# A two-layer MLP with per-row experts: the first chunks of the first layer by rows of x, with the weight loads spread over both queues

## The chip, the cores and the metric

The kernel runs on one NeuronCore of a Trainium2 chip. The metric is device time in microseconds (us), median over runs; an execution recorded by the hardware profiler gives the rows quoted here. Engines are named as in the profile: PE is the matrix engine (TensorE), PEld its weight loads, ACT ScalarE, DVE VectorE, POOL GpSimd, SP the sync engine, which here only issues transfers. SPq and ACTq are the transfers that SP and ACT issue.

## The reference

For 32 rows of x, each 256 tokens by 256 features, in fp32:

```python
h = gelu(einsum('bnd,hd->bnh', x, fc1_w) + fc1_b)         # HID = 1024, exact gelu
shared = einsum('bnh,sh->bns', h, fc2_w) + fc2_b          # 192 columns
We, be = experts_w[indices], experts_b[indices]           # one of 16 experts per row, 64 columns
expert_x = einsum('bnh,bph->bnp', h, We) + be[:, None, :]
return x + concatenate([shared, expert_x], axis=-1)
```

## The kernel before

Sixteen blocks of two rows of x (512 tokens) are worked on in turn. Hidden features lie in 8 chunks of 128. Every fp32 operand is split into two parts in a rounded fp32 format: a high part (HI), which ACT writes with a copy that rounds, and the rest (LO), which DVE or POOL writes as source minus HI. A product of two operands is three matmuls: HI HI, HI LO, LO HI. So each operand goes through a fixed relay: PE (or DVE, by 32x32 squares) transposes it into PSUM, ACT makes HI, DVE makes LO, and only then is it complete for PE.

Blocks 0 and 1 compute fc1 plainly, as 8 chunks each: a chunk is 2 halves of the features times 3 terms, 6 matmuls of 512 columns into one PSUM bank (`conv_chunk(c)`; `first_chunk()` for chunk 0 of block 0). Four banks are in turn, so chunk c waits for the gelu of chunk c-4. From block 2 on, fc1 runs in a Strassen-like scheme whose weight sums are made on POOL and DVE meanwhile. fc2 follows one pair of chunks behind: `fc2_first` for block 0, `fc2` later.

The order of work is written out by hand, one list for each engine, and each engine takes its list strictly in that order; semaphores join them. What counts for the change is the start:

- Loads. SP issues x of block 0 as two transfers (row 0, row 1; 256 KB each), waits for row 0, then issues the second half of fc1's weights (chunks 4 to 7, four strips of 128 KB), fc2's weights (`w2_piece`), the experts' rows and more. ACT issues the index, the first half of fc1's weights (chunks 0 to 3, four strips) and the bias b1.
- PE. `warm(20)` runs 20 matmuls on a constant, then 8 transposes of x (`x0_banks`; the PSUM banks are split by feature half, so both rows must be there before either bank is complete), `warm(10)`, 8 transposes of the first half of fc1_w (`w1_bank(0, d)`), b1, chunk 0, 8 transposes of the second half (`w1_bank(1, d)`), chunks 1 to 7, then `fc2_first(0)` (24 matmuls of 256 columns), then chunk 0 of block 1 (`conv_chunk(K)`).
- `fc2_first(0)` waits for `h_lo` (first pair of h split), for `e_lo` (experts' weights split, first half) and `w2_lo` 4 (all of fc2's weights split). `conv_chunk(K)` waits for `x1_lo` 2 (x of block 1 split).
- ACT and DVE make these splits between the gelus: `w1_high`/`w1_low`, `w2_square`, `w2_high`/`w2_low`, `both_experts_square`/`_high`/`_low`, `x_square`, `x1_high`/`x1_low`; `conv_high(q)` is the HI copy of h, one copy of 1024 elements for each pair of chunks.

In the trace, L1036 is `warm`, L1030 a transpose, L1074 `first_chunk`, L1067 `conv_chunk`, L1117 `fc2_first`; on ACT L456 x0_high, L469 w1_high, L479 w2_high, L498 both_experts_high, L510 x1_high, L560 the HI copy of h, L572 the gelu of a chunk; on DVE L716 w1_low, L739 w2_square, L747 w2_low, L775 and L782 the experts, L791 x_square, L808 x1_low, L886 to L891 drain_first, which frees fc2's accumulators for block 1.

## Time and profile before

| | |
|---|---|
| median of 3 runs | 360.57 us (360.05 to 361.18) |
| profiled execution, device time | 360.29 us |
| its span in the trace | 358.1 us |
| share of PE in the chain that ended last | 98% |
| PE busy / DVE / ACT / POOL | 98% / 73% / 69% / 66% |

Device time is the span and 2.2 us around it. The span is what the rows below describe, counted in us from its start. The busy time of PE is that of matmuls whose ends are modelled, so how far apart matmuls start says more than their durations.

### The profile page before, as it was taken

The numbers are of one execution on the slowest core, as the hardware profiler recorded it, in microseconds if no ns is written. First come the engines' busy times: TensorE is split into PE (matmuls) and PEld (weight loads), VectorE is DVE, ScalarE is ACT, GpSimd is POOL, SyncE is SP. The second block draws the span as 40 slices with busy tenths as digits, with TensorE's granted clock in tenths as the row PEclk, the third lists the DMA queues.
The fourth block names the chain that finished last, engine by engine and source line by source line (L and its number), as shares of the span: only waits on it lengthen the run. The fifth ranks groups of instructions, "written<-read, shape, count | busy, mean of one in ns | idle before, by whom it ended". The sixth has DMA issues, their size and how long they took to land.

```text
span 358.1 us, 7085 instructions
## 1 busy us (share of the span) xinstructions
PE 352.4 (98%) x2383; PEld 324.2 (91%) x2383; DVE 260.3 (73%) x500; ACT 246.6 (69%) x410; POOL 235.0 (66%) x150
## 2 busy tenths in 40 slices
PE   8999999999999999999999999999999999999995
PEld 6899899999999999999999999999999999999984
DVE  1797976977859698686968869697786959844543
ACT  3794957777677686776777678677767768656640
POOL 0079977858756587765758866586865658774570
PEclk9999999999999999999999999999999999999999
DMA  8969654524324333332533324234331231312001
GB/s 197 189 148 206 144 144 131 150 78 108 112 59 136 94 90 126 89 120 66 147 97 88 113 78 128 82 94 149 90 102 57 88 98 32 117 37 90 29 31 59
DMA packets 70061, 37.53 MB, mean 105 GB/s; under 512 B 43530, under 2 KB 70026, under 8 KB 70026
## 3 DMA queue, kind: packets, MB, share of 16 engines
q1 hardware_dynamic: 69408, 36.55, 38.0%
q10 hardware_dynamic: 618, 0.53, 0.6%
q8 instruction: 19, 0.31, 0.4%
q14 instruction: 16, 0.13, 0.1%
HBM read 28.68 MB, written 8.39 MB: 104 GB/s over the span
## 4 chain that ended last, share of the span: by engine, by line
PE 98%; DVE 0%; ACT 0%; issue 0%; POOL 0%; POOLq 0%; DVEq 0%
PE fc_ps L1091 39%; PE acc_ps L1147 30%; PE acc_ps L1150 15%; PE fc_ps L1067 6%; PE acc_ps L1117 3%; PE fc_ps L1036 2%; PE fc_ps L1147 1%; PE tr_ps L1030 1%; PE fc_ps L1150 1%; PE fc_ps L1074 1%; DVE resid L914 0%; ACT w1t L469 0%; PE acc_ps L1030 0%; POOL ident L416 0%; POOL ident L414 0%
## 5 line engine op out<-in xcount | busy, mean ns | idle before, releaser
L390 POOL TENSOR_TENSOR ht<-gelu,ht 128x1024 fp32r<-128x1024 f32 x62 | 149.5, 2412 | 98.8 <-ACT ht L560 98.8
L1147 PE MATMUL acc_ps<-w2t,ht 128*128 128x512 f32 x464 | 168.0, 396 | 0.0
L1091 PE MATMUL fc_ps<-xt,w1t 128*128 128x256 f32 x1176 | 159.6, 283 | 0.0
L1091 PEld LDWEIGHTS fc_ps<-xt,w1t 128*128 128x128 f32 x1176 | 148.6, 189 | 5.3
L1150 PE MATMUL acc_ps<-w2t,ht 128*128 128x256 f32 x464 | 130.0, 280 | 0.0
L1147 PEld LDWEIGHTS acc_ps<-w2t,ht 128*128 128x128 f32 x464 | 87.4, 188 | 16.0 <-POOL ht L390 0.3
L1150 PEld LDWEIGHTS acc_ps<-w2t,ht 128*128 128x128 f32 x464 | 87.8, 189 | 0.0
L560 ACT ACTIVATE ht<-gelu 128x1024 fp32r<-128x1024 f32 x64 | 68.0, 1063 | 3.3
L586 ACT ACTIVATE gelu<-work,b 128x512 f32<-128x512 f32 x56 | 37.3, 715 | 26.4 <-DVE work L865 26.2
L398 POOL TENSOR_TENSOR xt<-work,xt 128x1024 fp32r<-128x1024 f32 x14 | 33.8, 2415 | 14.9 <-ACT xt L549 14.9
L865 DVE TENSOR_TENSOR work<-fc_ps,work 128x512 f32<-128x512 f32 x28 | 19.4, 691 | 22.6 <-PE fc_ps L1091 21.3
L858 DVE TENSOR_TENSOR work<-fc_ps,work 128x512 f32<-128x512 f32 x28 | 19.1, 681 | 20.6 <-PE fc_ps L1091 20.6
L378 POOL TENSOR_TENSOR resid<-resid,bias 128x384 f32<-128x384 f32 x32 | 33.9, 1058 | 0.0
L489 ACT ACTIVATE w2t<-tr_ps 128x512 fp32r<-128x512 f32 x28 | 16.8, 599 | 24.6 <-DVE tr_ps L758 24.6
L539 ACT ACTIVATE work<-fc_ps 128x512 f32<-128x512 f32 x28 | 16.9, 602 | 21.8 <-PE fc_ps L1091 21.7
L914 DVE TENSOR_TENSOR resid<-acc_ps,resid 128x256 f32<-128x256 f32 x60 | 24.1, 422 | 8.2 <-PE acc_ps L1150 7.2
L873 DVE TENSOR_TENSOR work<-fc_ps,work 128x512 f32<-128x512 f32 x28 | 19.4, 691 | 13.2 <-PE fc_ps L1091 13.2
L795 DVE TENSOR_TENSOR work<-b_rows 128x256 f32<-128x256 f32 x14 | 27.7, 1976 | 1.2 <-ACT b_rows L530 1.1
L598 ACT ACTIVATE gelu<-work,b 128x256 f32<-128x256 f32 x56 | 25.4, 508 | 0.0
L907 DVE TENSOR_TENSOR resid<-acc_ps,resid 128x192 f32<-128x192 f32 x56 | 19.9, 355 | 6.8 <-PE acc_ps L1150 5.9
L603 ACT ACTIVATE gelu<-fc_ps,b 128x256 f32<-128x256 f32 x56 | 23.4, 475 | 0.0
L1067 PE MATMUL fc_ps<-xt,w1t 128*128 128x512 f32 x90 | 22.0, 392 | 0.0
(70 smaller groups left out, 326.6 us busy)
## 6 DMA issues: line engine op xcount, KB each, us to landing
pieces<-in_L_cond_experts_w SPq DMA_DIRECT2D x128, 64.0 KB, 2.0
out<-resid SPq DMA_DIRECT2D x32, 256.0 KB, 3.1
pieces<-in_x SPq DMA_DIRECT2D x60, 128.0 KB, 2.9
resid<-in_x SPq DMA_DIRECT2D x15, 512.0 KB, 3.5
e_bias<-in_L_cond_experts_b SPq DMA_DIRECT2D x32, 32.0 KB, 2.8
work<-in_L_cond_fc_w SPq DMA_DIRECT2D x4, 256.0 KB, 4.4
w_piece<-in_L_cond_fc_w SPq DMA_DIRECT2D x4, 192.0 KB, 5.2
resid<-in_x SPq DMA_DIRECT2D x2, 256.0 KB, 3.5
```

What stands on the lines that cost most here:

```text
L378: nc.gpsimd.tensor_tensor(rows[:, :, 0:SHARED], rows[:, :, 0:SHARED], bias[:, :].unsqueeze(1).to_broadcast([P, T, SHARED]), ALU.add).then_ ...
L390: nc.gpsimd.tensor_tensor(ht[:, slot, LO, :, :].rearrange("p k t -> p (k t)"), gelu[:, q % GELUS, :, :].rearrange("p k t -> p (k t)"), ht[ ...
L398: nc.gpsimd.tensor_tensor(xt[:, n % 2, X_T1:X_T4 + 1, LO, :], t_sum, xt[:, n % 2, X_T1:X_T4 + 1, HI, :].bitcast(FP32), ALU.subtract).then_ ...
L560: nc.scalar.activation(ht[:, q % SLOTS, HI, :, :].rearrange("p k t -> p (k t)"), gelu[:, q % GELUS, :, :].rearrange("p k t -> p (k t)"), A ...
L586: nc.scalar.activation(gelu[:, q % GELUS, j, :], upper[:, j, :], ACT.Gelu, bias=b1[:, k:k + 1]).then_inc(up_gelu, 1)
L598: nc.scalar.activation(gelu[:, q % GELUS, j, SEQ:2 * SEQ], c22[:, j, :], ACT.Gelu, bias=b1[:, k:k + 1]).then_inc(c22_gelu, 1)
L795: nc.vector.tensor_tensor(t_sum[:, o, :], in0, in1, ALU.subtract)\
L914: nc.vector.tensor_tensor(dst, src, dst, ALU.add).then_inc(drained, 1)
L1067: last = nc.tensor.matmul(fc1_ps[:, c % 4, :], conv_operand(k, d, w), xt_plain[c // K][:, d, v, :], start=(at == 0), stop=(at == len(terms ...
L1091: last = nc.tensor.matmul(fc1_ps[:, dst, j * SEQ:(j + 1) * SEQ], w1t[:, w, wv, ms], xt[:, n % 2, o, xv, :], start=(fresh and j == 0 and at ...
L1147: nc.tensor.matmul(acc.rearrange("p (v o) -> p v o", v=2), ht[:, q % SLOTS, HI, j, ts], w2t[:, :, k, fc2_columns(b)], start=(k == 0), stop ...
L1150: last = nc.tensor.matmul(acc[:, OUT:2 * OUT], ht[:, q % SLOTS, LO, j, ts], w2t[:, HI, k, fc2_columns(b)], start=False, stop=True, skip_gr ...
```

## The change

Only the start of the program is written anew.

- Loads: SP issues row 0 of x, then strips 0 and 1 of fc1's weights for chunks 0 and 1 (64 KB each), then four strips for chunks 2 and 3; ACT issues strips 2 and 3 for chunks 0 and 1 first, then row 1 of x, the index and b1. SP still waits for row 0 before the second half of the weights.
- PSUM banks are split by row of x and by chunk pair of the weights, not by feature half: `x0_banks(b)` fills one bank of row b with both feature halves, `w1_bank(half, l)` one bank with chunks 2l and 2l+1 of that half. The numbers of transposes (8 for x, 16 for fc1_w) and the sizes of the splits stay.
- PE: 12 warm matmuls instead of 20, and the 10 between x and the weights are gone. Chunks 0 and 1 are computed row by row (`first_chunk(c, b)`), 24 matmuls of 256 columns instead of 12 of 512. The transposes of the second half of the weights stand behind chunk 2.
- ACT: `conv_chunk(1)` stands between `w1_high(1, 0)` and `w1_high(1, 1)`; `conv_high(0)` stands ahead of `conv_chunk(2)`, where it stood behind `w2_high(3)`.
- DVE: the first two `w2_square` stand ahead of `w1_low(1, ...)`, where they stood behind.

```diff
-    WARM = 20
+    WARM = 12
...
-            for b in range(R):
-                ts = slice(b * T, (b + 1) * T)
-                sp.dma_start(resid[:, 0, ts, :], x_blocks[0][:, ts, :]).then_inc(x0_loaded[b], 16)
+            load_x0(sp, 0)
+            load_w1_pair(sp, 0, (0, 1))
+            load_w1_pair(sp, 1, range(Q))
...
+            load_w1_pair(act, 0, (2, 3))
+            load_x0(act, 1)
             act.dma_start(index_sb[:, :], index.rearrange("(o n) -> o n", o=1))\
                 .then_inc(index_loaded, 16)
-            load_w1(act, 0)
...
-            for d in range(D):
-                x0_high(d)
-            for d in range(D):
-                w1_high(0, d)
+            x0_high(0)
+            w1_high(0, 0)
+            x0_high(1)
+            w1_high(0, 1)
             act.wait_ge(b1_ready, 1)
             conv_chunk(0)
             w1_high(1, 0)
+            conv_chunk(1)
             w1_high(1, 1)
-            conv_chunk(1)
             w2_high(0)
             w2_high(1)
+            conv_high(0)
             conv_chunk(2)
             w2_high(2)
             conv_chunk(3)
             w2_high(3)
-            conv_high(0)
...
-            for d in range(D):
-                w1_low(1, d)
             w2_square(0)
             w2_square(1)
+            w1_low(1, 0)
+            w1_low(1, 1)
...
+            def first_chunk(c, b):
+                for at, (w, v, d) in enumerate([(w, v, d) for w, v in ((HI, HI), (HI, LO), (LO, HI))
+                                                for d in range(D)]):
+                    if c == 0 and at == 0:
+                        pe.wait_ge(w1_hi, 1)
+                        pe.wait_ge(x0_hi, b + 1)
+                    if c == 0 and (w, v, d) == (HI, LO, 0):
+                        pe.wait_ge(x0_lo, b + 1)
+                    if c == 0 and (w, v, d) == (LO, HI, 0):
+                        pe.wait_ge(w1_lo, 1)
...
             warm(WARM)
-            for b in range(R):
-                x0_banks(b)
-            warm(WARM // 2)
+            x0_banks(0)
             pe.wait_ge(w1_loaded[0], 16 * Q)
-            for d in range(D):
-                w1_bank(0, d)
+            w1_bank(0, 0)
+            x0_banks(1)
+            first_chunk(0, 0)
             pe.wait_ge(b1_loaded, 16)
             nc.tensor.transpose(fc1_ps[:, 3, 0:K], b1_in[:, :], ident[0:K, 0:K]).then_inc(b1_tr, 1)
-            first_chunk()
+            first_chunk(1, 0)
             pe.wait_ge(w1_loaded[1], 16 * Q)
-            for d in range(D):
-                pe.wait_ge(x0_lo, d + 1)
-                w1_bank(1, d)
-            conv_chunk(1)
+            w1_bank(0, 1)
+            first_chunk(0, 1)
+            first_chunk(1, 1)
+            pe.wait_ge(w1_lo, 2)
             conv_chunk(2)
+            pe.wait_ge(w1_loaded[2], 16 * Q)
+            pe.wait_ge(x0_lo, 2)
+            for l in range(2):
+                w1_bank(1, l)
             conv_chunk(3)
-            pe.wait_ge(w1_lo, 4)
+            pe.wait_ge(w1_lo, 3)
             conv_chunk(4)
             conv_chunk(5)
+            pe.wait_ge(w1_lo, 4)
```

PE's program from its first matmul to the end of fc2_first(0), before:

```order
L1036 MATMUL fc_ps<-ident 128x256 x20
L1030 MATMUL tr_ps<-ident,resid 128x128 x8
L1036 MATMUL fc_ps<-ident 128x256 x10
L1030 MATMUL acc_ps<-ident,w_in 128x128 x8
L1168 MATMUL fc_ps<-ident,b_in 128x8
L1074 MATMUL fc_ps<-xt,w1t 128x512 x6
L1030 MATMUL tr_ps<-ident,w_in 128x128 x8
L1067 MATMUL fc_ps<-xt,w1t 128x512 x42
L1117 MATMUL acc_ps<-w2t,ht 128x256 x24
```

and in the changed kernel, where L1046 is warm, L1040 a transpose, L1091 first_chunk, L1075 conv_chunk and L1130 fc2_first:

```order
L1046 MATMUL fc_ps<-ident 128x256 x12
L1040 MATMUL tr_ps<-ident,resid 128x128 x4
L1040 MATMUL acc_ps<-ident,w_in 128x128 x4
L1040 MATMUL tr_ps<-ident,resid 128x128 x4
L1091 MATMUL fc_ps<-xt,w1t 128x256 x6
L1180 MATMUL fc_ps<-ident,b_in 128x8
L1091 MATMUL fc_ps<-xt,w1t 128x256 x6
L1040 MATMUL acc_ps<-ident,w_in 128x128 x4
L1091 MATMUL fc_ps<-xt,w1t 128x256 x12
L1075 MATMUL fc_ps<-xt,w1t 128x512 x6
L1040 MATMUL tr_ps<-ident,w_in 128x128 x8
L1075 MATMUL fc_ps<-xt,w1t 128x512 x30
```

18 warm matmuls are gone (8 ahead of x, 10 ahead of the weights), and the last 8 transposes of weights have moved from behind chunk 0 to behind chunk 2.

ACT's program from the first split to the HI copies of the experts' weights, before:

```order
L456 ACTIVATE xt<-tr_ps 128x512 x2
L469 ACTIVATE w1t<-acc_ps 128x2x256 x2
L572 ACTIVATE gelu<-fc_ps,b 128x512
L469 ACTIVATE w1t<-tr_ps 128x2x256 x2
L572 ACTIVATE gelu<-fc_ps,b 128x512
L479 ACTIVATE w2t<-acc_ps 128x2x192 x2
L572 ACTIVATE gelu<-fc_ps,b 128x512
L479 ACTIVATE w2t<-acc_ps 128x2x192
L572 ACTIVATE gelu<-fc_ps,b 128x512
L479 ACTIVATE w2t<-acc_ps 128x2x192
L560 ACTIVATE ht<-gelu 128x1024
L572 ACTIVATE gelu<-fc_ps,b 128x512
L498 ACTIVATE w2t<-tr_ps 128x2x4x64 x2
```

and in the changed kernel (L481 x0_high, L485 w1_high, L496 w2_high, L577 the HI copy of h, L589 a gelu, L515 both_experts_high):

```order
L589 ACTIVATE gelu<-fc_ps,b 128x512
L485 ACTIVATE w1t<-tr_ps 128x2x256
L589 ACTIVATE gelu<-fc_ps,b 128x512
L485 ACTIVATE w1t<-tr_ps 128x2x256
L496 ACTIVATE w2t<-acc_ps 128x2x192 x2
L577 ACTIVATE ht<-gelu 128x1024
L589 ACTIVATE gelu<-fc_ps,b 128x512
L496 ACTIVATE w2t<-acc_ps 128x2x192
L589 ACTIVATE gelu<-fc_ps,b 128x512
L496 ACTIVATE w2t<-acc_ps 128x2x192
L589 ACTIVATE gelu<-fc_ps,b 128x512
L515 ACTIVATE w2t<-tr_ps 128x2x4x64 x2
```

The copy of 1024 elements stands two gelus and two w2_high earlier; the gelu of chunk 1 stands one w1_high earlier. Two x0_high and two w1_high stand in turn ahead of these rows.

DVE's program from the first split of weights to w2_low, before:

```order
L716 TENSOR_TENSOR w1t<-acc_ps,w1t 128x2x256 x2
L921 COPY b<-fc_ps 128x8
L716 TENSOR_TENSOR w1t<-tr_ps,w1t 128x2x256 x2
L739 STREAM_TRANSPOSE acc_ps<-w_piece 128x6x2x32 x2
L747 TENSOR_TENSOR w2t<-acc_ps,w2t 128x2x192
L739 STREAM_TRANSPOSE acc_ps<-w_piece 128x6x2x32
L747 TENSOR_TENSOR w2t<-acc_ps,w2t 128x2x192
L739 STREAM_TRANSPOSE acc_ps<-w_piece 128x6x2x32
L747 TENSOR_TENSOR w2t<-acc_ps,w2t 128x2x192 x2
```

and in the changed kernel (L726 w1_low, L749 w2_square, L757 w2_low):

```order
L726 TENSOR_TENSOR w1t<-acc_ps,w1t 128x2x256
L931 COPY b<-fc_ps 128x8
L749 STREAM_TRANSPOSE acc_ps<-w_piece 128x6x2x32 x2
L726 TENSOR_TENSOR w1t<-tr_ps,w1t 128x2x256 x2
L757 TENSOR_TENSOR w2t<-acc_ps,w2t 128x2x192
L749 STREAM_TRANSPOSE acc_ps<-w_piece 128x6x2x32
L757 TENSOR_TENSOR w2t<-acc_ps,w2t 128x2x192
L749 STREAM_TRANSPOSE acc_ps<-w_piece 128x6x2x32
L757 TENSOR_TENSOR w2t<-acc_ps,w2t 128x2x192 x2
```

The two w2_square that wait for the load of fc2's weights now stand ahead of the split of the second half of fc1's weights.

## Rows read from the trace of the kernel before

**Rows 1.** The page: span, and the chain that ended last by engine.

```profile
span 358.1 us, 7085 instructions
...
PE 98%; DVE 0%; ACT 0%; issue 0%; POOL 0%; POOLq 0%; DVEq 0%
```

**Rows 2.** Busy time by window: us, busy (count) of PE, PEld, DVE, ACT, POOL, granted clock, DMA, GB/s.

```profile
12.00:24.00 12.00, 12.00 (x65) 10.36 (x64) 10.72 (x19) 11.10 (x20) 4.83 (x2) 1.00 0.72 161
24.00:350.00 326.00, 326.00 (x2237) 302.27 (x2237) 243.48 (x465) 230.85 (x384) 229.43 (x142) 1.00 0.37 100
```

**Rows 3.** Timeline of PE, 0 to 24.9: start, us from first start to last end.

```profile
1.53 4.40 PE L1036 MATMUL fc_ps<-ident 128*128 128x256 bf16 x20 [1.53 <-POOL ident L416]
5.77 1.11 PE L1030 MATMUL tr_ps<-ident,resid 128*128 128x128 f32 x8
6.72 1.26 PE L1036 MATMUL fc_ps<-ident 128*128 128x256 bf16 x10
7.81 1.12 PE L1030 MATMUL acc_ps<-ident,w_in 128*128 128x128 f32 x8
...
9.14 1.83 PE L1074 MATMUL fc_ps<-xt,w1t 128*128 128x512 f32 x6
10.80 1.11 PE L1030 MATMUL tr_ps<-ident,w_in 128*128 128x128 f32 x8
11.66 9.81 PE L1067 MATMUL fc_ps<-xt,w1t 128*128 128x512 f32 x42
21.31 3.04 PE L1117 MATMUL acc_ps<-w2t,ht 128*128 128x256 f32 x24
24.18 1.09 PE L1067 MATMUL fc_ps<-xt,w1t 128*128 128x512 f32 x4
```

**Rows 4.** Timeline of ACT, 0 to 24.9.

```profile
6.74 1.09 ACT L456 ACTIVATE xt<-tr_ps 128x512 fp32r<-128x512 f32 x2 [1.72 <-PE tr_ps L1030]
...
16.91 0.49 ACT L479 ACTIVATE w2t<-acc_ps 128x384 fp32r<-128x384 f32 x1
17.30 1.05 ACT L560 ACTIVATE ht<-gelu 128x1024 fp32r<-128x1024 f32 x1
18.24 0.68 ACT L572 ACTIVATE gelu<-fc_ps,b 128x512 f32<-128x512 f32 x1
18.81 1.08 ACT L498 ACTIVATE w2t<-tr_ps 128x512 fp32r<-128x512 f32 x2
...
21.85 1.12 ACT L510 ACTIVATE xt<-tr_ps 128x512 fp32r<-128x512 f32 x2
```

**Rows 5.** Timeline of DVE, 0 to 24.9.

```profile
17.91 1.31 DVE L775 STREAM_TRANSPOSE tr_ps<-pieces 128x512 f32<-128x512 f32 x2
19.44 1.29 DVE L782 TENSOR_TENSOR w2t<-tr_ps,w2t 128x512 fp32r<-128x512 f32 x2 [0.22 <-ACT w2t L498]
20.77 1.32 DVE L791 STREAM_TRANSPOSE tr_ps<-pieces 128x512 f32<-128x512 f32 x2
22.52 1.29 DVE L808 TENSOR_TENSOR xt<-tr_ps,xt 128x512 fp32r<-128x512 f32 x2 [0.43 <-ACT xt L510]
```

**Rows 6.** Transfers of x, rows 0 and 1: duration of an issue, first and last start, landing.

```profile
L317 SPq DMA_DIRECT2D resid<-in_x x2: 443/450/458, 0.8 to 1.2; - x2
...
DMA to landing us min/median/max: 3.0/3.5/3.9
```

**Rows 7.** Transfers of fc1's weights; the landings are of all eight strips.

```profile
L267 ACTq DMA_DIRECT2D w_in<-in_L_cond_fc_w x4: 359/450/453, 1.3 to 2.7; - x4
...
DMA to landing us min/median/max: 3.2/4.1/4.3
```

**Rows 8.** Landing of fc2's weights (L322).

```profile
DMA to landing us min/median/max: 4.6/5.2/5.8
```

**Rows 9.** Timeline of all engines, 28 to 52: drain_first and block 1's fc2.

```profile
43.83 0.68 DVE L891 TENSOR_TENSOR resid<-acc_ps,resid 128x512 f32<-128x512 f32 x1
...
44.92 0.40 PE L1147 MATMUL acc_ps<-w2t,ht 128*128 128x512 f32 x1
```

More of the change, by code:

```diff
@@ L123, in cond_mlp_residual @@
         stored = [sem(f"stored{n}") for n in range(2)]
-        w1_loaded = [sem(f"w1_loaded{n}") for n in range(2)]
+        w1_loaded = [sem(f"w1_loaded{n}") for n in range(3)]
         w1p_loaded = sem("w1p_loaded")
@@ L262, in bank, with load_w1_pair, load_x0 @@
             return fc1_ps[:, i, :].rearrange("p (j t) -> p j t", j=2)
-        def load_w1(queue, half):
-            ks = slice(half * HALF, (half + 1) * HALF)
-            for q in range(Q):
-                queue.dma_start(w1_in[S * q:S * (q + 1), ks, :], w1_v[q][:, ks, :])\
-                    .then_inc(w1_loaded[half], 16)
+        def load_w1_pair(queue, l, strips):
+            for q in strips:
+                queue.dma_start(w1_in[S * q:S * (q + 1), 2 * l:2 * l + 2, :],
+                                w1_v[q][:, 2 * l:2 * l + 2, :]).then_inc(w1_loaded[l], 16)
+        def load_x0(queue, b):
+            ts = slice(b * T, (b + 1) * T)
+            queue.dma_start(resid[:, 0, ts, :], x_blocks[0][:, ts, :]).then_inc(x0_loaded[b], 16)
         block = ctx.enter_context(nc.Block())
@@ L1040, in x0_banks, with w1_bank @@
                 pe.wait_ge(x0_loaded[b], 16)
-                for d in range(D):
-                    last = transposes(tr_ps[:, d, b * SEQ:(b + 1) * SEQ],
-                                      [feature_chunk(resid[:, 0, b * T + t, :], d)
-                                       for t in range(T)])
-                    if b == R - 1:
-                        last.then_inc(x0_tr, 1)
-            def w1_bank(half, d):
-                transposes((acc_ps, tr_ps)[half][:, d, :], [
-                    feature_chunk(w1_in[:, k, :], d)
-                    for k in range(half * HALF, (half + 1) * HALF)]).then_inc(w1_tr, 1)
+                transposes(tr_ps[:, b, :], [
+                    feature_chunk(resid[:, 0, b * T + t, :], d)
+                    for d in range(D) for t in range(T)]).then_inc(x0_tr, 1)
+            def w1_bank(half, l):
+                k = half * HALF + 2 * l
+                transposes((acc_ps, tr_ps)[half][:, l, :], [
+                    feature_chunk(w1_in[:, k + j, :], d)
+                    for d in W1_ORDER[l] for j in range(2)]).then_inc(w1_tr, 1)
             def conv_operand(j, d, v):
@@ L1070, in conv_chunk @@
                 last.then_inc(conv_filled, 1)
[L1072 to L1084 removed]
+            def first_chunk(c, b):
[8 more added lines that the diff above has]
+                        pe.wait_ge(w1_lo, 1)
+                    last = nc.tensor.matmul(fc1_ps[:, c, b * SEQ:(b + 1) * SEQ],
+                                            conv_operand(c, d, w),
+                                            xt0[:, d, v, b * SEQ:(b + 1) * SEQ],
+                                            start=(b == 0 and at == 0), stop=True,
+                                            skip_group_check=True)
+                if b == R - 1:
+                    last.then_inc(conv_filled, 1)
             def product(n, g, dst, w, o, fresh):
```

80 lines of the change are left out of this document (34 added, 46 removed).

## The prediction

> **What bounds the kernel now.** First the chain that ended last: PE holds 98% of the span of 358.1 us [rows 1]. Then the busy time by window: from 12 to 350 us PE has no idle time at all, while DVE and ACT have some [rows 2]. So the time is the moment from which PE runs without a gap, plus a fixed amount of matmul work. That moment is 11.66, the first matmul of chunk 1 [rows 3]. Ahead of it the timeline of PE shows what lies on the path: warm matmuls from 1.53, x transposed at 5.77, ten more warm matmuls at 6.72 that cover the wait for weights, weights transposed at 7.81, chunk 0 at 9.14, the second 8 transposes at 10.80 [rows 3]. The profiled execution took 360.29 us, 0.28 below the median of 360.57; I work out a difference in its span and add it to the median.
>
> PE being without a gap doesn't say how near its helpers are behind. At two joints, the ends of rows of DVE stand against the starts of rows of PE. fc2_first(0) starts at 21.31 [rows 3] and needs the first split of the experts, which ends at 19.44 + 0.69 = 20.13 [rows 5]: 1.2 to spare. conv_chunk(K) starts at 24.18 [rows 3] and needs both splits of x of block 1, which end at 22.52 + 1.29 = 23.81 [rows 5]: 0.37 to spare. A third joint comes at 44.92, where fc2 of block 1 needs drain_first's last result, ready at 43.83 + 0.68 = 44.51 [rows 9]: 0.41 to spare. PE can therefore win no more than 0.4 at the start unless ACT and DVE get earlier too.
>
> **Prices.** From the distance of starts [rows 3]: 512 columns (11.66 to 21.31)/42 = 0.230 us; 256 columns (21.31 to 24.18)/24 = 0.120; a transpose (5.77 to 6.72)/8 = 0.119; b1 with its wait 9.14 - 8.86 is taken as 0.28 (8 transposes of 0.12 end at 8.8). Splitting 12 matmuls of 512 into 24 of 256 adds 24 x 0.120 - 12 x 0.230 = 0.12. Warm matmuls: (4.40 - 0.4)/19 = 0.21 in the first group, (1.26 - 0.27)/9 = 0.11 in the second. Granted clock reads 1.00, but 256 columns in 0.213 us are 1.2 GHz and in 0.107 us 2.4 GHz, so PE worked at the lower level through the first group, to about 5.6, and at the higher after it; ahead of the rise lay 4 us of unbroken matmuls. On ACT [rows 4], one of 512 elements lasts 0.60 and the next starts 0.49 after it (1.09 for two), 384 elements: next after 0.39, gelu 0.57 (18.24 to 18.81), the HI copy of h 0.94 (17.30 to 18.24). On DVE 0.7 for 512 elements and the next 0.6 after (1.3 for two) [rows 5]. Handing over costs about 0.05 each time.
>
> **Landings.** Row 0 of x landed 3.0 after its issue at 0.75, row 1 3.9 after 1.25, so 3.75 and 5.15; the first four strips of weights (issued 1.3 to 2.7) landed by 2.7 + 4.3 = 7.0, with 1 MB in all [rows 6, 7]. In the changed kernel the first 512 KB are row 0 and the weights of chunks 0 and 1, so these weights land between 3.75 and 5.15; I take 4.6. Row 1 ends the first 768 KB, between 5.15 and 7.0: 5.7. Chunks 2 and 3 end the first 1 MB: 7.0.
>
> **The start, step by step.** Twelve warm matmuls end at 1.53 + 12 x 0.213 = 4.1. Four transposes of row 0 and two of weights fall before 5.6 or about there. At the lower clock no row shows a transpose; bounds are 0.12 (no slower) and 0.24 (twice); I take 0.24, as the warm matmuls doubled. So row 0 is transposed by 5.05, the weights by 5.75, row 1 (landed) by 6.25. ACT: x0_high(0) from 5.3, w1_high(0,0) 6.0 to 6.6; PE starts chunk 0 at 6.65 after a wait of 0.4. DVE's w1_low(0,0) ends at 7.35, so the last two matmuls of that row wait 0.15 and end at 7.7. Then b1 8.0, chunk 1's row 8.7, four transposes 9.2, 12 matmuls 10.65. The relay for chunks 2 and 3 (transposed 9.35, HI 9.95, LO 10.7) lets chunk 2 start at 10.75; before, chunk 2 started at 11.66 + 6 x 0.23 = 13.04. Here the second 8 transposes still stand ahead (0.96), so PE has won 13.04 - 10.75 - 0.96 = 1.3. Undisturbed it would reach fc2_first at 10.75 + 0.1 (a restart) + 36 x 0.23 + 0.96 = 20.1, where it was 21.31.
>
> **What ACT and DVE do with it.** The second w1 bank pair is what they need next, and it isn't earlier but later: chunk 2 ends at 12.25, four transposes at 12.75, so w1_high(1,0) starts at 12.9; before, the weights were transposed from 10.80 on [rows 3] and it followed chunk 0's gelu. ACT takes its list in order, so nothing behind it can pass. From 12.9 the list runs without a gap: 0.49 + 0.57 + 0.49 + 0.39 + 0.39 + 0.94 + 0.57 + 0.39 + 0.57 = 4.8 until the last w2_high starts at 17.7 and ends at 18.2; before it ended at 16.91 + 0.49 = 17.40 [rows 4]. The HI copy of h that now stands ahead of it (0.94) is what makes it so late. DVE started the experts' squares 0.51 after that end (17.91) [rows 5]; now 18.7. First square done 19.4, ACT's HI 19.45 to 20.05, second HI to 20.7, DVE's first LO 20.1 to 20.8. PE, there at 20.1, waits 0.7. Its 24 matmuls end at 20.85 + 0.1 + 2.88 = 23.85. Meanwhile ACT: gelu 20.6, HI copy 21.15, gelu 22.1, x1_high 22.7 and 23.2; DVE: x squares from 21.5 (first done 22.2), x1_low 23.3 and 23.9, done 24.6. PE waits another 0.8 and starts conv_chunk(K) at 24.65 instead of 24.18: **+0.47**, and +0.1 because the matmul after a wait is followed 0.1 late (the loading of its weights is not hidden; 9.14 to 10.80 is 1.66 for six matmuls worth 1.38, with two or three waits in it [rows 3]). The drain's joint: DVE is later by about 0.85 (x squares of block 2), PE by 0.57, so 0.28 of the 0.41 is used and nothing added, give or take 0.1. Sum: **+0.6**, 360.57 + 0.6 = 361.2, and 360.9 for the profiled execution.
>
> DVE's squares of fc2's weights now stand in front of w1_low(1,0). They need the load that landed by 7.0 + 5.8 = 12.8 [rows 8]; SP gets there 0.3 to 0.4 later (two more issues of 0.45 and one less ahead), but the bytes ahead are the same, so 12.8 to 13.2. They end at 13.9 to 14.3, ACT's w1_high(1,0) long before. Chunk 4 waits for w1_low(1,0), done 14.55 to 15.0, and PE is there at 14.6: up to 0.4 more wait here, but it comes off the wait at fc2_first. Edits that cost nothing: b1 lands long before 7.7; POOL's first HI/LO step comes earlier than before.
>
> **Rivals.**
> First, the clock rises late (slower). PE has 8 warm matmuls fewer early and none in the middle, with waits near 5.1 and 6.3 to 6.65. If that keeps it at the lower level, work between 5.6 and that moment T takes twice its time. Up to 7 the relay's waits absorb it; from then each us costs 0.5. With T = 8: +0.5 more, 361.7; T = 9: +1.0 more, 362.2. Past the bound for "slower" (+1.08) from T = 8. For it: 0.21 against 0.11 per warm matmul in the rows shows how much is at stake. Against it: up to 5.1 PE is as busy as before, and 4 us of work were enough. The Trainium skill ("TensorE: Matmul & The Clock Gate", Part 1: The HAM clock gate) has it that half rate is the default and activity releases it, which speaks against thinning the warm-up; by that rule alone the case above, 361.7 to 362.2, would be the likeliest. The trace agrees that PE starts at half rate; whether thinner activity delays the rise no row here shows.
> Second, nothing waits (faster). If ACT and DVE kept up, PE's 1.2 would stay: 359.4. For it: row 0's relay starts earlier than anything did before. Against: it needs the experts' split by 20.1, where the list gives 20.8, and x1_low by 23.0, where it gives 24.6. One move in order won't find 1.6 us.
> Third, loads are later than taken. Weights of chunk 0 at 5.6 and row 1 at 6.5 instead of 4.6 and 5.7 would shift all by 0.4; fc2's weights at 14 by 0.7 more: 361.6 to 362.3.
> Fourth, the transposes at the lower clock cost 0.12, not 0.24: six of them save 0.5, partly on ACT: +0.2, 360.8, no change.
>
> **How the numbers follow.** Forecast (+0.2 to +1.0, split losses and stalls as above, the fourth case in it) 0.62; late clock 0.18; late loads 0.12; nothing waits 0.08. A change of 0.3%, 1.08 us, is about what a measurement of this kernel can tell from no change. The forecast lies within it but for a tenth (0.06 slower); of the late clock 0.12 is slower, of late loads 0.07; of the last case half is faster. So faster 0.05, same 0.70, slower 0.25. Likeliest 361.2; the range leaves out the last case and the ends of the second and third: 360.0 to 362.2.
>
> **What would show it.** PE starts x's transposes near 4.1, chunk 0 near 6.7, conv chunk 2 near 10.8; PE waits for DVE ahead of fc2_first for 0.4 to 0.9 and ahead of conv_chunk(K) for 0.6 to 1.0, and starts the latter between 24.4 and 25.0. ACT stands idle for 1.5 before w1_high(1,0) near 12.9. Wrong if these two waits are missing, if matmuls past 6 start 0.24 apart at 256 columns, or if a wait shows near 45.

## The result and the profile after

| | before | after |
|---|---|---|
| median of 12 runs each, same chip | 360.62 us | 362.64 us |
| range | 359.73 to 361.37 | 361.25 to 364.41 |
| profiled execution: device time, span | 360.29, 358.1 | 362.88, 360.6 |
| chunk 2 starts, in that execution | 13.04 | 12.56 |
| `conv_chunk(K)` starts | 24.18 | 26.42 |

The ratio is 1.0055 with a 95% interval of 1.0037 to 1.0072: slower by 2.0 us. Forecast was 361.2, "no change", in a range of 360.0 to 362.2; the forecast and its range missed. The profiled span grew by 2.5, of which 2.24 are there at the start of `conv_chunk(K)`. Two runs of the kernel before, taken beside the last experiment at a lower granted clock (0.85 and 0.56), are left out of every comparison.

PE's timeline in the changed kernel's trace, to be held against [rows 3] (start, us from first start to last end):

```profile
1.53 2.74 PE L1046 MATMUL fc_ps<-ident 128*128 128x256 bf16 x12 [1.53 <-POOL ident L441]
4.38 1.13 PE L1040 MATMUL tr_ps<-ident,resid 128*128 128x128 f32 x4
6.09 1.13 PE L1040 MATMUL acc_ps<-ident,w_in 128*128 128x128 f32 x4 [0.58 <-DMA w_in<-in_L_cond_fc_w]
7.01 1.06 PE L1040 MATMUL tr_ps<-ident,resid 128*128 128x128 f32 x4
7.90 1.65 PE L1091 MATMUL fc_ps<-xt,w1t 128*128 128x256 f32 x6
9.49 0.27 PE L1180 MATMUL fc_ps<-ident,b_in 8*128 8x8 f32 x1
...
12.56 1.66 PE L1075 MATMUL fc_ps<-xt,w1t 128*128 128x512 f32 x6
14.06 1.11 PE L1040 MATMUL tr_ps<-ident,w_in 128*128 128x128 f32 x8
14.92 7.09 PE L1075 MATMUL fc_ps<-xt,w1t 128*128 128x512 f32 x30
22.69 3.10 PE L1130 MATMUL acc_ps<-w2t,ht 128*128 128x256 f32 x24 [0.68 <-issue]
26.42 1.67 PE L1075 MATMUL fc_ps<-xt,w1t 128*128 128x512 f32 x6 [0.63 <-DVE xt L818]
```

Read it in two parts. From chunk 2 on, things go as worked out: 26.42 - 12.56 = 13.86 from chunk 2 to `conv_chunk(K)`, where the prediction has 24.65 - 10.75 = 13.90, with PE stopped ahead of fc2_first (the last matmul starts at 21.62, the next at 22.69) and again ahead of `conv_chunk(K)` (25.51 to 26.42). Both stops are about 0.8 longer than the pace explains. Ahead of chunk 2 it went otherwise: chunk 2 was to start at 10.75 and started at 12.56. PE waits for the weights of chunk 0 until 6.09, which were to be there at 4.6. And the six matmuls at 7.90 take 1.59 to the next start.

ACT's and DVE's timelines of the same stretch, against [rows 4, 5]:

```profile
14.72 0.60 ACT L485 ACTIVATE w1t<-tr_ps 128x512 fp32r<-128x512 f32 x1 [1.42 <-PE tr_ps L1040]
...
17.00 1.09 ACT L577 ACTIVATE ht<-gelu 128x1024 fp32r<-128x1024 f32 x1
...
19.46 0.55 ACT L496 ACTIVATE w2t<-acc_ps 128x384 fp32r<-128x384 f32 x1
...
24.44 1.09 ACT L527 ACTIVATE xt<-tr_ps 128x512 fp32r<-128x512 f32 x2
```

```profile
20.51 1.31 DVE L785 STREAM_TRANSPOSE tr_ps<-pieces 128x512 f32<-128x512 f32 x2
...
25.08 1.29 DVE L818 TENSOR_TENSOR xt<-tr_ps,xt 128x512 fp32r<-128x512 f32 x2 [0.54 <-ACT xt L527]
```

ACT is idle for 1.42 until the second half's weights are transposed (forecast 1.5), starts the last w2_high 4.74 after w1_high(1,0) (forecast 4.8), and DVE's experts' squares follow 1.05 later. The relay is the one that was described, moved later as a whole.

The loads, by the views of two source lines (L286 issues the strips for chunks 0 to 3 of fc1's weights, L291 the rows of x), against [rows 6, 7]:

```profile
L286 SPq DMA_DIRECT2D w_in<-in_L_cond_fc_w x6: 419/434/473, 1.2 to 3.7; - x6
L286 ACTq DMA_DIRECT2D w_in<-in_L_cond_fc_w x2: 441/444/448, 0.7 to 1.2; - x2
...
DMA to landing us min/median/max: 2.7/3.9/4.3
```

```profile
DMA to landing us min/median/max: 3.6/4.0/4.4
```

The first of the two views is of the strips, the second of the rows of x. A strip of 64 KB takes 2.7 to 4.3 us to land, hardly less than the strips of 128 KB did (3.2 to 4.3). The four strips for chunks 0 and 1 landed at 3.4, 4.5, 5.0 and 6.0, row 0 at 4.34 (before: 3.75) and row 1 at 6.14; the strips for chunks 2 and 3, last of the first 1 MB, at 7.55 (before, where they are those for chunks 0 to 3: 6.98).

### The profile page after: what moved, and what is told of

Same layout as the page of the kernel before. It is cut to its first block, busy times and chain, and to the rows that moved or that the text cites. A ratio compares the mean times of both kernels' runs of the same rounds, so it can differ in the third digit from the quotient of the medians.

```text
span 360.6 us, 7080 instructions
## 1 busy us (share of the span) xinstructions
PE 353.0 (98%) x2377; PEld 324.3 (90%) x2377; DVE 260.5 (72%) x500; ACT 246.6 (68%) x410; POOL 235.1 (65%) x150
## 4 chain that ended last, share of the span: by engine, by line
PE 94%; ACT 3%; DMA 1%; DVE 1%; issue 0%; SPq 0%; DVEq 0%
PE fc_ps L1104 39%; PE acc_ps L1160 30%; PE acc_ps L1163 15%; PE fc_ps L1075 4%; PE acc_ps L1130 2%; DMA w_in<-in_L_cond_fc_w 1%; PE fc_ps L1160 1%; PE fc_ps L1091 1%; ACT gelu L589 1%; ACT ht L577 1%; PE fc_ps L1163 1%; DVE resid L924 0%; PE acc_ps L1040 0%; ACT w2t L496 0%; PE tr_ps L1040 0%; DVE xt L818 0%
## 5 line engine op out<-in xcount | busy, mean ns | idle before, releaser
L577 ACT ACTIVATE ht<-gelu 128x1024 fp32r<-128x1024 f32 x64 | 68.0, 1062 | 3.6 <-issue 0.4
L620 ACT ACTIVATE gelu<-fc_ps,b 128x256 f32<-128x256 f32 x56 | 23.4, 475 | 0.0
L1075 PE MATMUL fc_ps<-xt,w1t 128*128 128x512 f32 x84 | 21.1, 396 | 0.6 <-DVE xt L818 0.6
```

The source lines that it names most:

```text
L577: nc.scalar.activation(ht[:, q % SLOTS, HI, :, :].rearrange("p k t -> p (k t)"), gelu[:, q % GELUS, :, :].rearrange("p k t -> p (k t)"), A ...
L1075: last = nc.tensor.matmul(fc1_ps[:, c % 4, :], conv_operand(k, d, w), xt_plain[c // K][:, d, v, :], start=(at == 0), stop=(at == len(terms ...
```

## The experiments

All were timed against the kernel before on the same chip; "beyond the span" is device time less span. `conv_chunk(K)` is the last place of the start at which PE waits, where it waits at all, so its start is the number to watch. Where one span is given for a kernel, it is the median of its own runs; two numbers are the shortest and the longest. The ratios in brackets and their 95% intervals are those of the comparison of all runs; where runs scatter they differ from the quotient of the two medians (for the changed kernel timed again 1.0055, where 362.05 over 360.92 is 1.0031). So a difference in ratio of 0.001, 0.4 us, is not to be read from two kernels that scatter. The theory after the first two traces was: the landings (+0.8) and the clock (up to +1.1) moved chunk 2, and the place of the second 8 transposes makes ACT and DVE follow. The rival was that the new order of ACT and DVE is itself the loss.

**Second half's transposes ahead of chunk 2.**

```diff
             first_chunk(1, 1)
-            pe.wait_ge(w1_lo, 2)
-            conv_chunk(2)
             pe.wait_ge(w1_loaded[2], 16 * Q)
             pe.wait_ge(x0_lo, 2)
             for l in range(2):
                 w1_bank(1, l)
+            pe.wait_ge(w1_lo, 2)
+            conv_chunk(2)
```

> The changed kernel with the transposes of the second half of fc1's weights put ahead of chunk 2 instead of behind it; nothing else. Theory 'late relay': the split lists of ACT and DVE start with these transposes, so w1_high(1,0) starts about 1.5 us earlier (near 13.2 instead of 14.7), the waits ahead of fc2_first and of conv_chunk(K) move forward with it, and the time is 1.2 to 1.6 us below the changed kernel, 361.0 to 361.4. Rival 'late start': what counts is only when PE starts on the weights (6.09) and how fast it works there; the order behind it is covered, the time stays at 362.6 within 0.4.

Measured: 361.21 (ratio 1.0025, 1.0009 to 1.0040), spans 358.1 to 359.2, 1.3 under the changed kernel's median span. PE and DVE in its trace:

```profile
12.22 8.45 PE L1075 MATMUL fc_ps<-xt,w1t 128*128 128x512 f32 x36
20.56 3.11 PE L1130 MATMUL acc_ps<-w2t,ht 128*128 128x256 f32 x24
24.29 1.66 PE L1075 MATMUL fc_ps<-xt,w1t 128*128 128x512 f32 x6 [0.63 <-DVE xt L818]
```

```profile
12.96 1.05 DVE L749 STREAM_TRANSPOSE acc_ps<-w_piece 128x384 f32<-128x384 f32 x2 [1.47 <-DMA w_piece<-in_L_cond_fc_w]
13.93 1.26 DVE L726 TENSOR_TENSOR w1t<-tr_ps,w1t 128x512 fp32r<-128x512 f32 x2
```

The wait ahead of fc2_first is gone. The one ahead of `conv_chunk(K)` stays, and DVE shows why: it is idle for 1.47 until fc2's weights land, since their squares stand at the head of its list, and then has no gap until x1_low, ahead of which it waits 0.54 for ACT. Here the bound is that landing plus the list behind it, 24.29 - 12.96 = 11.3.

**Warm matmuls between row 0 and the weights.**

```diff
-    WARM = 12
+    WARM = 14
+    FILL = 4
...
             x0_banks(0)
+            warm(FILL)
```

> The changed kernel with 14 warm matmuls instead of 12 and 4 more between the transposes of row 0 and those of the weights, so that PE has no idle time before 6 us; nothing is shorter by that. Theory 'thin activity': the clock then rises near 5.8 as before the change instead of at 9.7, matmuls of 256 columns are 0.12 apart from 8 us on, and the time falls by about 1.0 us to 361.6, with a spread like that of before (1.6 us) instead of 3.2. Rival 'moment by chance': the rise isn't tied to the idle time, the profile may show any moment between 5.5 and 9.7, and median and spread stay at 362.6 and 3.

Measured: 362.41 (1.0054, 1.0040 to 1.0067), from five runs. The expected gain of 1.0 did not come: the ratio is that of the changed kernel. But the spans lie between 359.6 and 360.2 only, where the changed kernel's go from 359.0 to 361.3; that half of the theory held. Chunk 2 starts at 11.52, and the clock has risen by 5.8. So with the late clock out of play there still is a loss: the median span, 360.1, is 1.8 above that of the kernel before on this chip. The recorded run, the shortest of the five, shows 1.5 of it, 1.2 of that at the start of `conv_chunk(K)`, from landings and relay; what the other four runs lose besides is not seen.

**Row 1 of x issued last.**

```diff
-            load_x0(act, 1)
             act.dma_start(index_sb[:, :], index.rearrange("(o n) -> o n", o=1))\
                 .then_inc(index_loaded, 16)
...
+            load_x0(act, 1)
```

> The changed kernel with row 1 of x issued last on ACT's queue, behind the index and b1. Theory 'late loads': row 1's 256 KB travelled beside SP's second strip and held it back to 6.04; issued 1.1 us later they don't, the weights of chunk 0 land near 5.0, PE starts on them 1 us earlier, and the time falls by 0.4 to 0.6 us at a clock that rises as late as before, to 362.1. Rival: the strip is late for its own place in SP's queue, it lands at 5.8 to 6.0 all the same, row 1 lands later (6.8), and the time is 362.6 to 363.

Measured: 362.56 (1.0061, 1.0043 to 1.0079). The weights of chunk 0 land at 5.10 instead of 6.04, but row 1 at 7.06 instead of 6.14, and chunk 2 starts at 11.53. A load that is put back gives its place to another, and chunks 0 and 1 need both. Two of the six spans (360.9 and 361.0) stand 1 us above the other four.

**The new order of ACT and DVE in the kernel before.** The two lists of the change, PE and loads as before:

```diff
             w1_high(1, 0)
-            w1_high(1, 1)
             conv_chunk(1)
+            w1_high(1, 1)
             w2_high(0)
             w2_high(1)
+            conv_high(0)
...
             w2_high(3)
-            conv_high(0)
...
-            for d in range(D):
-                w1_low(1, d)
             w2_square(0)
             w2_square(1)
+            for d in range(D):
+                w1_low(1, d)
```

> The kernel before with the new order on ACT and DVE alone (gelu of chunk 1 ahead of w1_high(1,1), the HI copy of h ahead of chunk 2's gelu, two w2_square ahead of w1_low(1,0)). Theory 'order costs': the last w2_high ends about 0.9 later, conv_chunk(K) waits 0.4 for x1_lo where it had 0.37 to spare, the time rises by 0.3 to 0.5 us to 361.0. Rival 'order is free': PE keeps its 0.37 to spare, 360.6.

Measured: 360.94 against 360.55 (1.0016, 1.0007 to 1.0024), so +0.4. `conv_chunk(K)` waits for x1_low here: the last matmul ahead of it starts at 24.60, it starts at 25.08. The rival is right in kind and small in size: the order costs 0.4 of 2.0.

This trace shows something else as well. PE's start is that of the kernel before, and yet:

```profile
5.77 1.63 PE L1030 MATMUL tr_ps<-ident,resid 128*128 128x128 f32 x8
7.24 1.25 PE L1036 MATMUL fc_ps<-ident 128*128 128x256 bf16 x10
...
12.20 9.81 PE L1067 MATMUL fc_ps<-xt,w1t 128*128 128x512 f32 x42
```

The eight transposes of x take 1.47 to the next start, where they took 0.95, and chunk 1 starts at 12.20 instead of 11.66 [rows 3]. The transposes start 0.213 apart until 6.84, so the clock rose there and not near 5.7. Of the 0.90 by which `conv_chunk(K)` is later than before in this trace, 0.54 are this. With the full warm-up, too, the moment of the rise moves.

**The same warm-up in a program of the old length.** The comparison of device times left something that no span shows. Beyond the span, the kernel before takes 2.1 to 2.4 us in each of its runs; the changed kernel takes 2.2 to 2.4 in seven runs and 2.9 to 3.8 in five. What differs near the end of the two traces is q8, a queue of instruction fetches of 16 KB each; I take it for PE's, since its place changes with the length of PE's program. Its last transfer lies at 347 in the trace of before. After, nothing of that queue shows there, and it comes at 361.5 to 362.6, behind the last instruction of the span (360.6). Window 345 to 350 of before, then window 360 to 363 of the changed kernel:

```profile
q8 instruction: 1, 0.02, 1.2%
```

```profile
DMA packets 2, 0.02 MB, mean 8 GB/s; under 512 B 0, under 2 KB 0, under 8 KB 0
## 3 DMA queue, kind: packets, MB, share of 16 engines
q8 instruction: 1, 0.02, 2.2%
```

The recorded run of the first experiment (transposes ahead of chunk 2) took 3.25 beyond its span; there the fetch lies at 361.0 to 361.9 and the span ended at 358.4, so it ended 3.5 behind the span. In the changed kernel's recorded run it ended 2.0 behind, and that run has 2.28 beyond its span, no more than the kernel before. The change made PE's program six matmuls shorter. So:

```diff
-            def warm(times):
+            def warm(times, cols=2 * P):
...
-            warm(WARM)
+            warm(18, 170)
```

> [...] Theory of the code fetch: in the runs of the kernels with the shorter program so far, PE's last fetch of instructions lies at the program's end (about 361 us) and the device time beyond the span is 2.7 to 3.9 us in 5 of 12; here the last fetch is back near 348 and that part is 2.1 to 2.5 in every run. Median down by 0.3 to 0.4, to about 362.3; spans as those of the changed kernel (359.0 to 361.3), chunk 2 from 12.2 on if the clock rises early, 12.6 if late. Rival, that the part beyond the span has nothing to do with the length of the code: some of the runs again over 2.7.

Measured: 361.86 (1.0051, 1.0031 to 1.0071); beyond the span 2.27 to 2.36 in all ten runs; the last fetch at 348; spans 358.9 to 362.3, median 359.55. Nearly the same columns in six more instructions take the tail away. Spans still scatter: three of ten are 1 us or more above the others, and the interval is too wide to show the gain in the median.

**Fewer warm matmuls in the kernel before, in a shorter program and in one of the old length.**

```diff
-            warm(WARM // 2)
+            warm(4)
```

> The kernel before with 4 warm matmuls instead of 10 between x and fc1's weights, nothing else. These ten end at 7.8 and the weights had landed by 7.0, so PE starts their transposes near 7.15 instead of 7.81. The joint ahead of conv_chunk(K) has 0.37 to spare, but here ACT and DVE get the weights earlier too, so all moves: span -0.6, about 357.6. But PE's program is shorter by six matmuls: by the theory of the code fetch its last fetch comes at the end, and in some of the runs the device time beyond the span is over 2.7. Median 360.0 to 360.3 with the tail, runs up to 361. Rival, that the ten matmuls keep the clock up: a rise past 7 and no gain or a loss.

and with `warm(26, 196)` for `warm(WARM)` besides:

> The same as the last, and the 20 warm matmuls of 256 columns in the first group are 26 of 196 (5096 columns for 5120), so that PE's program is as long as before. Span -0.6, last fetch near 348, device time beyond the span 2.1 to 2.5 in all runs, median 359.9 to 360.0. By the rival on the code fetch it equals the last one.

Measured: 360.46 (0.9997, 0.9983 to 1.0011) and 360.08 (0.9988, 0.9979 to 0.9997), against 360.59. Beyond the span: over 2.9 in three of twelve runs of the first, 2.14 to 2.38 in all eleven of the second; last fetch at 359 and at 347. Median spans 358.15 and 357.8, before 358.2. The gain in the span is 0.4 in the second and next to nothing in the first, where 0.6 was expected of both. In the two traces the clock rose late, near 6.5: x's transposes took 1.29 and 1.25 to the next start, where they took 0.95 [rows 3]. So the four warm matmuls behind them end late, and the weights' transposes start at 7.51 and 7.43, where 7.15 was expected.

**Three edits in the changed kernel:** the warm matmuls of the second run, the transposes of the first, and the HI copy of h back at its old place.

```diff
             w2_high(1)
-            conv_high(0)
             conv_chunk(2)
...
             w2_high(3)
+            conv_high(0)
```

> The changed kernel with three edits: 14 warm matmuls and 4 more between row 0 and the weights (PE's program is then as long as before), the transposes of the second half of the weights ahead of chunk 2 instead of behind it, and the HI copy of h back behind the last w2_high. The second edit alone took off 1.4 us; the third lets the last w2_high end 0.9 earlier than it did, and the wait ahead of fc2_first with it, though conv_chunk(K) waits for the sum of ACT's and DVE's lists, which the copy only changes places in, so it brings 0 to 0.4 there. Theory (relay and landings are the loss): about as the kernel before, 360.4 to 361.0, wait ahead of fc2_first under 0.3, device time beyond the span 2.1 to 2.5. If the clock were a loss of its own that these edits don't touch, 361.2 or more.

Measured: 361.11 (1.0015, 1.0007 to 1.0024), spans 358.5 to 359.1. That is 0.1 beyond what was expected at most, and one part of it was wrong: a wait ahead of fc2_first is there, 20.22 to 21.43, where under 0.3 was expected.

```profile
17.85 1.05 ACT L578 ACTIVATE ht<-gelu 128x1024 fp32r<-128x1024 f32 x1
...
18.98 2.39 POOL L416 TENSOR_TENSOR ht<-gelu,ht 128x1024 fp32r<-128x1024 f32 x1 [17.50 <-ACT ht L578]
...
21.43 3.12 PE L1131 MATMUL acc_ps<-w2t,ht 128*128 128x256 f32 x24 [0.82 <-POOL ht L416]
```

The releaser is POOL: it needs 2.4 us for h's LO after ACT's copy. This joint was in the kernel before too, with 0.47 to spare (POOL is done at 18.43 + 2.41 = 20.84, fc2_first starts at 21.31), and the prediction doesn't have it. It explains what the copy's early place is good for, and by how much it may slip: it must start 3.6 ahead of fc2_first (1.05 + 0.1 + 2.4).

**The warm-up of the change alone, in the kernel before.**

```diff
-            warm(WARM)
+            warm(30, 102)
...
-            warm(WARM // 2)
```

> [...] All loads, orders of ACT and DVE and the rest stay. Warm matmuls end near 4.1, PE is idle until row 1 of x has landed (about 5.1), then 8 transposes, idle until the weights land (about 7.0), 8 transposes, chunk 0. If a thinner warm-up as such makes the clock rise late (my first rival), the rise comes at 8 to 9.5 in most runs, chunk 0's matmuls start 0.43 apart, and the span is up by 0.5 to 1.0 against the run with 4 warm matmuls between (357.8), so 358.3 to 358.8 and more spread among runs. If it doesn't, the span is that run's less up to 0.1 (the weights landed just now set the start): 357.7, device time 360.0.

Measured: 360.49 (0.9995, 0.9982 to 1.0008), and the median says nothing here: the twelve spans lie in two groups, six from 357.4 to 357.7 and six from 358.6 to 359.0. A loss of 1.0 in half of the runs is what the rival of the late clock would make. But it is not shown: the kernel before's own 29 runs on this chip have spans from 357.7 to 359.2, so the second group is no longer than runs with the full warm-up, and the first is merely as short as the best of them. One recorded run can't show both groups; it is of the first:

```profile
4.06 2.23 PE L1030 MATMUL tr_ps<-ident,resid 128*128 128x128 f32 x8
6.91 1.22 PE L1030 MATMUL acc_ps<-ident,w_in 128*128 128x128 f32 x8 [0.62 <-DMA w_in<-in_L_cond_fc_w]
```

All of x's transposes are at the lower clock here (0.213 apart), and those of the weights, behind the wait, at the higher (0.12).

**The changed kernel again.**

> The changed kernel once more, unaltered, on this chip, for a second sample of what varies from run to run. Expected: spans of 359.0 to 361.3, in some runs about 1 longer because the clock rises late; device time beyond the span over 2.7 in about 4 of 12; the last fetch of PE's instructions at the end of the program. Median 362.3 to 362.7. If the late clock of the recorded run was a rare accident, the rise is near 5.5 here and the span 359.3.

Measured: 362.05 (1.0055, 1.0030 to 1.0080), six of twelve runs over 2.7 beyond the span, eight spans from 358.9 to 359.9 and four from 360.9 to 362.4. This recorded run has the early clock, which makes it the counterpart of the first one:

```profile
5.87 0.74 PE L1040 MATMUL acc_ps<-ident,w_in 128*128 128x128 f32 x4 [0.64 <-DMA w_in<-in_L_cond_fc_w]
6.45 0.64 PE L1040 MATMUL tr_ps<-ident,resid 128*128 128x128 f32 x4
7.30 1.23 PE L1091 MATMUL fc_ps<-xt,w1t 128*128 128x256 f32 x6 [0.21 <-ACT w1t L485]
8.46 0.22 PE L1180 MATMUL fc_ps<-ident,b_in 8*128 8x8 f32 x1
...
11.49 1.65 PE L1075 MATMUL fc_ps<-xt,w1t 128*128 128x512 f32 x6
...
25.34 1.66 PE L1075 MATMUL fc_ps<-xt,w1t 128*128 128x512 f32 x6 [0.62 <-DVE xt L818]
```

From start to next start, the four transposes of weights take 0.58 instead of 0.92 and the six matmuls 1.16 instead of 1.59; chunk 2 starts at 11.49 instead of 12.56 and `conv_chunk(K)` at 25.34 instead of 26.42. The two recorded runs are 1.07 apart at chunk 2 and 1.08 at `conv_chunk(K)`, so the difference arrives in full at the end of the relay. Not all of it is the clock: 0.22 are there at the start of the weights' transposes (6.09 for 5.87), since the last strip landed at 6.04 and here at 5.83. The clock's part is 0.85.

**The second half's relay brought forward on all three engines** (with the warm matmuls as in the second run).

```diff
             w1_bank(0, 1)
+            pe.wait_ge(w1_loaded[2], 16 * Q)
+            pe.wait_ge(x0_lo, 2)
+            for l in range(2):
+                w1_bank(1, l)
             first_chunk(0, 1)
...
+            w1_high(1, 0)
+            w1_high(1, 1)
             act.wait_ge(b1_ready, 1)
             conv_chunk(0)
-            w1_high(1, 0)
             conv_chunk(1)
-            w1_high(1, 1)
...
-            w2_square(0)
-            w2_square(1)
             w1_low(1, 0)
             w1_low(1, 1)
+            w2_square(0)
+            w2_square(1)
```

> In the changed kernel the relay of the second half of fc1's weights is brought ahead of the landing of fc2's weights on all three engines: PE transposes them right behind those of chunks 2 and 3, ahead of the second row of chunks 0 and 1; ACT makes their HI ahead of the first two gelus; DVE makes their LO ahead of fc2's squares. 14 warm matmuls and 4 between row 0 and the weights keep the program's length and the clock. Theory: with the transposes ahead of chunk 2 (run e1) DVE was idle for 1.5 before fc2's weights landed at 13.0 and then had no gap until conv_chunk(K), at 24.29, so the landing of fc2's weights plus DVE's list was the bound. Taking the two splits (1.26) out of that list lets x of block 1 be split by 23.2, and PE reaches conv_chunk(K) undisturbed at 20.5 + 2.95 = 23.45 to 23.6: span -0.7 to -0.8 against e1's 358.5, about 357.7, device time 360.0, and 0.5 under the kernel before. Rival, that the landings and PE's own start are all there is to win: 358.4 as before, with another wait (POOL's LO of h, or the experts' split) in its place.

Measured: 360.58 (0.9992, 0.9982 to 1.0002), spans 357.9 to 358.8, `conv_chunk(K)` at 23.76. The median span is 0.3 under the first experiment's, or 0.6 if each is held against the kernel before on its own chip (358.3 and 358.6), for 0.7 to 0.8 expected; at `conv_chunk(K)` the trace shows 0.5 (24.29 to 23.76). In its trace ACT's copy of h starts at 14.38 and its third w2_high at 15.90, though the square was done at 15.24, and DVE waits 0.40 for the fourth: with the weights early, the copy's new place would be what delays the list; the next run tests that.

**And the copy back at its old place.** The diff is that of the run with three edits.

> The last kernel, with the HI copy of h (1024 elements on ACT, 0.94 to the next start) back behind the last w2_high. In the last run it stood at 14.38, and made ACT's third w2_high start at 15.90 where its square was done at 15.24; DVE waited 0.4 for the fourth. Theory: the copy's place ahead of the w2_highs costs 0.5 in DVE's list as soon as the weights no longer come late. Without it the experts' squares start near 17.35 (17.86), x of block 1 is split by 23.2, and PE reaches conv_chunk(K) undisturbed at 20.4 + 3.0 = 23.4 (23.76): span -0.3 to -0.4, 357.8, device time 360.1 to 360.2. Rival: the copy then starts at 16.8 or later, and POOL, which needs 0.1 + 2.4 from its end for the LO of h, is done only at 20.3 or later, so PE waits for POOL ahead of fc2_first as in the run with three edits; from a copy start of 17.0 on this eats the gain.

Measured: 360.13 (0.9989, 0.9981 to 0.9998), spans 357.5 to 358.1, all device times between 359.74 and 360.37.

```profile
16.77 1.05 ACT L578 ACTIVATE ht<-gelu 128x1024 fp32r<-128x1024 f32 x1
...
17.91 2.41 POOL L416 TENSOR_TENSOR ht<-gelu,ht 128x1024 fp32r<-128x1024 f32 x1 [16.43 <-ACT ht L578]
...
20.46 3.04 PE L1131 MATMUL acc_ps<-w2t,ht 128*128 128x256 f32 x24
...
23.34 0.96 PE L1076 MATMUL fc_ps<-xt,w1t 128*128 128x512 f32 x3
```

POOL ends at 20.32 and PE starts fc2_first at 20.46 without a wait; `conv_chunk(K)` follows at 23.34 (expected 23.4), without one either. From chunk 2 to there PE has no gap. By the traces the copy's place cost 0.4 (23.76 to 23.34); the ratios, 0.9992 and 0.9989 on two chips, are too close to show it. This version, built from the change, and the one with fewer warm matmuls in the kernel before (at the old length) are the only two whose interval lies below 1, and only just (up to 0.9998 and 0.9997): 0.4 and 0.5 us under the medians of before on their chips, 360.49 and 360.59.

## Why the prediction was wrong

**The frame held.** The time is the moment from which PE runs without a gap; behind `conv_chunk(K)` the span is 0.3 longer (334.2 for 333.9), of which the 0.1 of the restart was taken; at the drain's joint PE doesn't wait. ACT's and DVE's answer (w1_high(1,0) 4.8 ahead of the last w2_high, experts, x of block 1, the two waits of 0.7 and 0.8) was right to 0.1: 13.86 against 13.90 from chunk 2 to `conv_chunk(K)`. That PE's win would be lost because the second bank pair is late was right too: with the transposes ahead of chunk 2 the median span falls by 1.3.

**The landings failed.** "In the changed kernel the first 512 KB are row 0 and the weights of chunks 0 and 1, so these weights land between 3.75 and 5.15; I take 4.6": they landed at 6.04, beyond the upper bound. The bound was taken as if bytes landed in the order of their issue, at the rate of before. But row 0 itself landed 0.6 later than before, now with strips of the other queue in flight from the first, and the last of the four strips landed 4.3 after its issue, as a strip of twice the size did. Row 1 was taken at 5.7 and landed at 6.14, chunks 2 and 3 at 7.0 and 7.55. In the traces with an early clock (the changed kernel again, and the run with 18 warm matmuls), in which the weights landed at 5.83 and 5.79, chunk 2 starts at 11.49 and 11.45 for the 10.75 of the prediction, so this term is worth +0.7, and in the first recorded run, where they landed 0.2 later, +0.9. It was rival three, with a price of 0.4 and a chance of 0.12: both too small. What in the new load pattern makes the first 1 MB 0.6 later (ten transfers in place of six, or two queues started together) no run settles; the run with row 1 last shows only that it can't be shifted away.

**The clock, the first rival, came in part.** The first recorded run lost 0.85 by it, and its matmuls show it: 256 columns start 0.213 apart up to 9.14. The rival's price was too high: with a rise near 9.7, 0.5 for each us past 7 makes 1.3, but part of the slow work falls into time in which PE waits for ACT at the early clock: from the transposes of row 1 to chunk 0 it takes 0.89 in one recorded run and 0.85 in the other. It isn't the likeliest case either. In 34 runs of the changed kernel and of its twin of the old length, 11 spans are 360.6 or more and 23 are 359.9 or less; that this gap is the clock is read from the two recorded runs of the changed kernel (359.6 with the early clock, 360.6 with the late one), not from each run. With warm matmuls in the gap between row 0 and the weights (four kernels, 40 runs) there is no second group. There is none either in the 12 runs of the first experiment, without such matmuls; there the landing of fc2's weights and the list behind it bind, and may hide it.

The prediction held against the rival that "up to 5.1 PE is as busy as before". That was no safeguard. PE starts nothing from 5.1 to 6.1, since the weights are late. But this gap alone doesn't decide: the second recorded run has it too (4.95 to 5.87), and its transposes had drawn together ahead of it, at 4.84. Nor is the full warm-up one: with the start of before, matmuls are slow up to 5.6 in one trace and up to 6.8 in another, and the kernel before scatters over 1.5 us itself. Why the same program falls once on this side and once on that, no run shows. The Trainium skill ("TensorE: Matmul & The Clock Gate", Part 1: The HAM clock gate) has the default at half rate and lets activity release it. The traces agree with the first half: the warm matmuls of 256 columns start 0.213 apart in every one that has them. That thinner activity releases it later fits the 11 long runs of 34 against none of 40, and the kernel before with the thin warm-up doesn't show it (ratio 0.9995). The fourth rival was wrong: transposes at the lower clock started 0.213 apart, close to the 0.24 that was taken and not at its 0.12.

**The tail was not in the prediction at all.** "I work out a difference in its span and add it to the median" takes what lies beyond the span as fixed. Five of the changed kernel's twelve runs took 0.6 to 1.5 more there than the others; over all 24 runs the mean is 2.72 against 2.32 before, +0.4. Shown: it goes with the length of PE's program. The four kernels whose program is six matmuls shorter have it in 20 of 54 runs; the eight whose program is as long as before have it in none of 85, and the kernel before itself in none. Two pairs differ in nothing else but a few columns of warm-up: the changed kernel and its twin, on different chips (11 of 24 runs, none of 10), and, on one chip, the kernel before with fewer warm matmuls and its twin (3 of 12, none of 11). Shown as well: in the recorded runs of the shorter programs the last fetch comes at 356 to 362 instead of 346 to 348. That this fetch makes the tail is a guess: the one recorded run with a tail (3.25 beyond it) is also the one in which the fetch ended far behind the span (3.5), while in the other four it ended 2.1 behind it at most and there is no tail. Why a shorter program asks for it so late was not tried.

**The sum as measured.** +0.6 as forecast, +0.7 from landings, 0.85 in a third of the runs (+0.3 on average), +0.4 on average from the tail: 2.0, and the measured number is +2.0. That it comes out is in part luck. The run with the four warm matmuls between has neither tail nor late clock and should stand 1.3 above before, but its five spans do by 1.8; 0.5 of that stays open. Waits and order were read rightly; the landing of the first weights and the part beyond the span, taken as safe, were not.

## What to carry to other kernels

When loads are cut smaller and spread over more queues to have a first piece sooner, don't let the piece land by its share of the bytes: take the duration from issue to landing of the nearest transfer in the trace as it stands, for small ones too, and let those that share its time become later. Bring forward what the second wave of the relay needs before anything else of the start; a win of PE alone is paid back at the next two joints. And look at the runs one by one: a median in which two groups stand 1 us apart, or a part of the time that lies outside the span, is not found in one recorded execution.

## What the runs showed of the hardware

- Device time can change with the length of PE's program alone: with a program six matmuls shorter, 20 of 54 runs took 0.4 to 1.6 us more beyond the span, and none of 85 at the old length. The last fetch of instructions lies at 356 to 362 instead of 346 to 348.
- The moment at which TensorE's clock rises from 1.2 to 2.4 GHz differs from run to run of one program: 256 columns started 0.213 apart until 9.1 in one run of the changed kernel and 0.12 apart from 7.5 on in another. The granted clock of both stretches reads 1.00 in the view by windows; only the distance of starts tells.
- A transfer of 64 KB took 2.7 to 4.3 us to land, one of 128 KB 3.2 to 4.3, with 1 MB under way on two queues.
